# Routing of two expert layers: raw rows gathered and normalised tile by tile, picks in two parts, one-hot products of ids alone

## The chip, the cores and the metric

One NeuronCore of a Trainium2 chip runs the whole program; nothing is exchanged with other cores. Its engines are TensorE (PE, with its weight loads as PEld), VectorE (DVE), ScalarE (ACT), GpSimd (POOL) and SyncE (SP). SP and POOL mostly issue DMAs. The metric is the device time of one execution in microseconds, as the median of several runs.

## The reference

Two layers, each a graph attention over 3327 nodes of 256 features and then a mixture of eight experts, each added to x. Only the second half of a layer matters here:

```python
# layer 0: h = layernorm(x), H = 512
logits = h @ gate_w + gate_b;  probs = softmax(logits)
top2_vals, top2_idx = top_k(probs, 2)
x = x + sum over e of cw[:, e] * (gelu(h @ W1[e] + b1[e]) @ W2[e] + b2[e])     # cw: the two values, 0 elsewhere
# layer 1: xt = layernorm(x), normalised a second time per token, H = 1024
top_p, top_idx = top_k(softmax(xt @ Wr + br), 2);  weights = top_p / top_p.sum()
xe = xn * ln_g[e] + ln_b[e]
x = x + sum over the two picks of weight * (gelu(xe @ W1[e] + b1[e]) @ W2[e] + b2[e])
```

## The kernel before, in words

The nodes are padded to 3328 rows, held in X as T = 26 row tiles of 128 rows (PAIRS = 13 pairs). Attention fills X. Then the class `Experts` does, in each layer, **routing** and the **run of tiles**.

Routing (`route_tensor`, `route_scalar`, `route_vector`, `route_sync`) goes through these stages:

- *Gates.* For each row tile PE turns 128 rows (L2165, two transposes), ACT copies the turned tile out of PSUM (L2128), and PE multiplies it by the gate weights into 8 columns of bank 2 (L2173). Two buffers alternate, so PE turns tile t before it multiplies tile t - 1. After each tile PE does two products that nobody reads (`idle_products`, L2180). ACT's square root for the layer norm (L2432) stands after the tenth tile in ACT's order and needs the variance from DVE (L2424). Meanwhile DVE normalises all of X in place, tile by tile (L2008), and SP stores the result to the DRAM tensor `xs` in two halves (L1966), between the first and the last four of eight loads of the second expert weights W2.
- *Picks.* DVE takes all 26 x 8 logits, finds the two largest of each row with a chain of 17 instructions (L2021 to L2038), each waiting for the one before it (`step`). PE fills the time with 48 unread products, then counts rows per expert (L2189, L2190).
- *Places.* From the counts DVE works out for each pick the tile (of 59) and the place in it (of 128): L2040 to L2065. PE does 96 unread products.
- *One-hots.* The 52 columns of picks go in four quarters c of 13. For each, DVE compares tile numbers (L2102, 13 x 59), compares places (L2107, 13 x 128) and multiplies the first by the row ids (L2111); ACT multiplies the first by the pick's weight (L2151, 13 instructions). PE's 13 products (L2199) put ids and weights side by side, 118 columns, into bank 5. Between the second and the third quarter DVE makes the table of each tile's expert (L2081 to L2087); on it wait the loads of W1. DVE turns bank 5 into `slot_row` (L2118, L2120) and copies the weights to `slot_w` (L2122).

The run has 59 tiles (RUN_TILES). POOL gathers 128 rows of `xs` into one of four `rx` buffers (L2255), PE turns them (L2292), ACT copies (layer 0, L2340) or scales (layer 1, L2344), PE does the hidden products (L2285), ACT the gelu (L2362), PE the second product (L2324), DVE adds the bias and multiplies by the weight (L2388, L2391), and POOL adds the rows to DRAM (L2273). SP loads W1 of tile g + 2 (L2215) once tile g's hidden products are done. In PE's order tile g means: hidden products of g + 1, turning of g + 2, second product of g. The bias b2 (L2225) is loaded once both first gathers have landed, because it lies where X was.

In layer 0 a loop on SP (`gelu_sync`, L1344) stores each finished pair of X to `xd`; in layer 1 `route_sync` stores X to `out` when most of the rows are final (L1953).

## Time and profile before

| | us |
|---|---|
| median of 3 runs (1788.11 to 1790.72) | 1789.14 |
| the profiled execution | 1787.74 |
| its span, first to last instruction | 1786.0 |
| PE busy / DVE busy / ACT busy / POOL busy | 1660.1 / 931.6 / 955.8 / 351.8 |
| mean granted TensorE clock, share of full speed | 0.981 |
| layer 0: gates, picks, places, one-hots (422.5 to 481.4) | 58.9 |
| layer 1: the same stages (1281.9 to 1342.4) | 60.5 |

The profiled execution's own time is 1.74 us longer than its span and 1.4 us shorter than the median. A stage below is a stretch of the span; "busy" in it is the time in which an engine had an instruction. PE counts as busy during the unread products too, so its share does not say where time can be saved.

### The profile page before, as it was taken

The numbers are of one execution on the slowest core, as the hardware profiler recorded it, in microseconds if no ns is written. First come the engines' busy times: TensorE is split into PE (matmuls) and PEld (weight loads), VectorE is DVE, ScalarE is ACT, GpSimd is POOL, SyncE is SP. The second block draws the span as 40 slices with busy tenths as digits, with TensorE's granted clock in tenths as the row PEclk, the third lists the DMA queues.
The fourth block names the chain that finished last, engine by engine and source line by source line (L and its number), as shares of the span: only waits on it lengthen the run. The fifth ranks groups of instructions, "written<-read, shape, count | busy, mean of one in ns | idle before, by whom it ended". The sixth has DMA issues, their size and how long they took to land.

```text
span 1786.0 us, 41369 instructions
## 1 busy us (share of the span) xinstructions
PE 1660.1 (93%) x13364; PEld 1535.9 (86%) x13365; DVE 931.6 (52%) x2186; ACT 955.8 (54%) x2194; POOL 351.8 (20%) x314
## 2 busy tenths in 40 slices
PE   4799999999799999589999999999988999999998
PEld 3588888878789999479999999999978999999997
DVE  4578868778612222568888878877780111111111
ACT  1143444435334433368989989899743444444443
POOL 2110000000156666320000000000002333333332
PEclk9899999999899999799999999999999999999999
DMA  9990000003478887400000000000375666666664
GB/s 160 108 176 10 10 10 9 28 28 125 143 190 208 229 209 186 159 10 18 14 14 19 9 19 18 10 19 14 110 281 175 176 177 179 182 186 186 176 176 97
DMA packets 86495, 189.98 MB, mean 106 GB/s; under 512 B 13737, under 2 KB 60585, under 8 KB 77577
## 3 DMA queue, kind: packets, MB, share of 16 engines
q1 hardware_dynamic: 53705, 139.39, 23.5%
q0 software_dynamic: 31360, 48.45, 17.2%
q10 hardware_dynamic: 1344, 1.05, 0.2%
q8 instruction: 47, 0.77, 0.2%
q14 instruction: 39, 0.32, 0.1%
HBM read 188.98 MB, written 33.11 MB: 124 GB/s over the span
## 4 chain that ended last, share of the span: by engine, by line
PE 52%; DVE 3%; ACT 1%; issue 1%; DMA 1%; DVEq 0%; POOL 0%; ACTq 0%; POOLq 0%
PE bank L1774 24%; PE bank L2285 12%; PE bank L2324 11%; PE bank L707 1%; PE bank L710 1%; PE bank L2292 1%; ACT arena L1476 1%; DVE arena L1612 0%; PE bank L2173 0%; PE bank L697 0%; DVE arena L1610 0%; DMA arena<-xe 0%; DVE X L2107 0%; PE bank L2180 0%; PE bank L2165 0%
## 5 line engine op out<-in xcount | busy, mean ns | idle before, releaser
L1774 PE MATMUL bank<-arena 128*128 128x195 bf16 x5408 | 467.1, 248 | 14.2 <-DVE arena L1612 10.9
L1774 PEld LDWEIGHTS bank<-arena 128*128 128x128 fp8e4 x5408 | 463.8, 97 | 17.6 <-issue 16.7
L1476 ACT ACTIVATE arena<-arena,m_row 128x512 fp8e5<-128x512 f32 (+1 forms) x672 | 401.5, 678 | 44.5 <-DVE arena L1612 32.8
L2285 PEld LDWEIGHTS bank<-X,arena 128*128 128x128 f32 x2832 | 337.1, 194 | 8.7 <-issue 2.3
L2388 DVE TENSOR_TENSOR arena<-bank,X 128x256 f32<-128x256 f32 x118 | 50.1, 425 | 563.7 <-PE bank L2324 563.7
L2285 PE MATMUL bank<-X,arena 128*128 128x128 f32 x2832 | 339.2, 277 | 0.1
L2324 PE MATMUL bank<-arena,X 128*128 x1416 | 325.2, 379 | 2.5 <-ACT X L2362 2.0
L1319 PE MATMUL bank<-arena 128*128 (+1 forms) x1352 | 312.1, 386 | 15.1 <-DVE arena L1225 15.1
L1319 PEld LDWEIGHTS bank<-arena 128*128 128x128 f32 x1352 | 252.5, 191 | 55.7 <-issue 20.9
L2324 PEld LDWEIGHTS bank<-arena,X 128*128 128x128 f32 x1416 | 259.9, 190 | 33.7 <-issue 3.1
L2362 ACT ACTIVATE X<-bank,arena 128x128 f32<-128x128 f32 x708 | 196.0, 379 | 70.2 <-issue 61.5
L1177 ACT ACTIVATE bank<-arena,s_all 128x384 f32<-128x384 f32 (+1 forms) x234 | 133.7, 573 | 185.7 <-DVE arena L1217 182.7
L1217 DVE SCALAR_TENSOR_TENSOR arena<-arena,d_all,bank 128x384 f32<-128x384 f32 (+1 forms) x234 | 140.8, 602 | 67.9 <-PE bank L1319 66.7
L2344 ACT ACTIVATE X<-bank,arena 128x128 f32<-128x128 f32 x118 | 47.6, 454 | 226.8 <-PE bank L2292 226.8
L2207 POOL IOTA arena<- 128x128 f32 x2 | 0.5, 238 | 808.4 <-DVEq L1674 495.0
L1610 DVE SCALAR_TENSOR_TENSOR arena<-arena 128x512 uint32<-128x512 uint32 (+1 forms) x168 | 109.7, 653 | 73.4 <-PE bank L1774 53.9
L2273 POOL DMA_INDIRECT out<-X,slot_row x59 | 93.4, 1583 | 269.2 <-DVE X L2391 266.2
L2255 POOL DMA_INDIRECT arena<-xs,slot_row x118 | 116.3, 986 | 146.6 <-DVE slot_w L2122 111.2
L1225 DVE TENSOR_TENSOR arena<-arena 128x384 f32<-128x384 f32 (+1 forms) x234 | 126.9, 546 | 0.0
L1612 DVE SCALAR_TENSOR_TENSOR arena<-arena 128x512 uint32<-128x512 uint32 (+1 forms) x168 | 108.9, 648 | 0.0
L2340 ACT COPY X<-bank 128x256 f32<-128x256 f32 x59 | 22.0, 373 | 105.0 <-PE bank L2292 105.0
L2292 PE MATMUL bank<-ident,arena 128*128 128x128 f32 x236 | 46.2, 278 | 11.5 <-DMA arena<-xs,slot_row 9.0
(249 smaller groups left out, 1346.2 us busy)
## 6 DMA issues: line engine op xcount, KB each, us to landing
arena<-m1w SPq DMA_DIRECT2D x67, 1024.0 KB, 10.6
arena<-m0w SPq DMA_DIRECT2D x67, 512.0 KB, 7.1
xs<-X SPq DMA_DIRECT2D x4, 1664.0 KB, 7.1
arena<-qd SPq DMA_DIRECT2D x25, 256.0 KB, 3.1
arena<-adjT POOLq DMA_DIRECT2D x13, 448.0 KB, 12.9
arena<-adjT POOLq DMA_DIRECT2D x13, 384.0 KB, 10.8
xe<-zeros POOLq DMA_DIRECT2D x1, 3456.0 KB, 21.7
X<-x_in SPq DMA_DIRECT2D x2, 1664.0 KB, 11.5
```

Source lines behind the costliest of these rows:

```text
L1177: a.activation(self.exp_bank[s][:, 0:nt * P], self.rows[r][:, 0:nt * P], ACT.Exp, bias=s_all[:, at(c, 1)]).then_inc(self.exp_ready[s], 1)
L1217: v.scalar_tensor_tensor(out=self.prob[q][:, 0:w], in0=self.rows[r][:, W:W + w], scalar=d_all[:, at(c, 1)], in1=self.exp_bank[s][:, 0:w], ...
L1225: v.tensor_tensor(self.prob[q][:, 0:w], self.prob[q][:, 0:w], mask[:, at(c * NP + b * W, w)], ALU.min).then_inc(self.prob_ready[q], 1)
L1319: last = pe.matmul(bank[3 * r + n][:, 0:D + 1], self.prob[q][:, n * P:(n + 1) * P], V[:, at(c * VW, D + 1)], start=False, stop=False, skip ...
L1476: last = a.activation(self.sign[slot].bitcast(F8W)[:, q * W:q * W + nt * P], self.row[r][:, 0:nt * P], ACT.Sigmoid, scale=STEEP, bias=self ...
L1610: v.scalar_tensor_tensor(out=pos, in0=sg, scalar=1, in1=m, op0=ALU.logical_shift_left, op1=ALU.bitwise_and).then_inc(self.pos_ready, 1)
L1612: v.scalar_tensor_tensor(out=neg, in0=sg, scalar=0x08080808, in1=m, op0=ALU.bitwise_xor, op1=ALU.bitwise_and).then_inc(self.neg_ready[slot ...
L1774: last = pe.matmul(bank[rb * NT + n][:, kind * KW:(kind + 1) * KW], self.split[slot][kind].bitcast(F8)[:, q * W + n * P:q * W + (n + 1) * ...
L2255: pool.indirect_dma_start(self.rx[g % 4], None, xs[:, :], bass.IndirectOffsetOnAxis(ap=slot_row[:, g:g + 1], axis=0)).then_inc(self.rx_loa ...
L2285: last = pe.matmul(bank[2 * s + c // 4][:, c % 4 * P:(c % 4 + 1) * P], self.W1[s][:, k * HID + c * P:k * HID + (c + 1) * P], self.rxt[s][: ...
L2324: last = pe.matmul(bank[5 + s][:, 0:D], self.ht[s][:, c * P:(c + 1) * P], self.W2[:, at(e * (HC * D) + c * D, D)], start=(c == 0), stop=(c ...
L2362: last = a.activation(self.ht[s][:, c * P:(c + 1) * P], bank[2 * s + c // 4][:, c % 4 * P:(c % 4 + 1) * P], ACT.Gelu, bias=self.b1[:, at(e ...
```

## The change

- `norm` of X in place (L2008) and its stores are gone. SP stores the raw rows to `xs`: in layer 0 a second store beside each store to `xd`; in layer 1 in three parts (12, 12 and 2 tiles), each together with a store to `out`, the first as soon as three blocks of rows are final.
- A row of `xs` grows from 256 to 260 words (ROW): four words `row_cols` hold the row's scale and shift, the first pick's weight, and the second's minus the first's. They are stored by one DMA in 16-byte pieces, once `weights()` is done.
- DVE normalises each gathered tile in the run (`norm`), two instructions, three tiles ahead; PE turns a tile after that.
- Picks are found in two parts, tiles 0 to 19 and 20 to 25; the second part's logits go to bank 7.
- The one-hot products carry ids alone, 59 columns. Of 13 id products DVE does 3 (in one instruction), ACT 10. A second pick's id is raised by 4096, from which DVE reads afterwards whether a slot is a second pick.
- The table of experts moves behind the last quarter, `weights()` from the first to the second quarter.
- The two unread products after each gate are gone; 48 become 20 and 96 become 88.

```diff
@@ gelu_sync (layer 0)
                     sp.dma_start(xd[...], X[...]).then_inc(self.x_kept, 16)
+                    sp.dma_start(xs[at(i * 2 * P, 2 * P), 0:D].rearrange("(t p) d -> p t d", p=P),
+                                 X[...]).then_inc(rows_stored, 16)
@@ route_sync
-                    for a, b, final in ((0, T - 2, 6), (T - 2, T, 7)):
+                    for a, b, final in ((0, 12, 3), (12, 24, 6), (24, T, 7)):
                         sp.wait_ge(rows_final, final)
+                        sp.dma_start(xs[a * P:b * P, 0:D]..., X[...]).then_inc(self.rows_stored, 16)
                         sp.dma_start(total[a * P:b * P, :]..., X[...]).then_inc(self.x_spilled, 16)
...
-                load_w2(range(4))
-                for g in range(2):
-                    sp.wait_ge(self.x_scaled, (g + 1) * PAIRS)
-                    sp.dma_start(xs[...], X[...]).then_inc(self.xn_stored[g], 16)
-                load_w2(range(4, 8))
+                for g in range(8):
+                    sp.dma_start(self.W2[...], w2m[...]).then_inc(self.w2_loaded, 16)
+                sp.wait_ge(self.weights_ready, 1)
+                sp.dma_start(xs[0:NP, D:ROW].rearrange("(t p) c -> p t c", p=P), self.row_cols
+                             ).then_inc(self.cols_stored, 16)
@@ route_vector
-                with v.Fori(0, PAIRS) as i:
-                    for s in range(2):
-                        v.tensor_scalar(xv, xv, self.scale_x[...], self.shift_x[...], ALU.mult, ALU.add)
+                for (a, b), logits_bank in zip(PICK_PARTS, (bank[2], bank[7])):
+                    pick_part(a, b, logits_bank)
...
+                v.wait_ge(*x_stored)
+                v.wait_ge(self.rows_stored, self.n_stored)
                 for c in range(4):
...
-                    v.tensor_tensor(tiles_[:, :, 0, :], eq, over(ids, G), ALU.mult)
+                    v.tensor_tensor(self.hot_tile[b][:, 0:few * G]..., eq[:, 0:few, :],
+                                    over(ids[:, first:first + few], G), ALU.mult)
-                    if c == 1:
-                        tile_table()
+                tile_table()
...
-                v.tensor_copy(slot_w[:, :], bank[5][:, G:2 * G])
+                step(v.tensor_scalar(slot_w[:, :], slots, float(SECOND), None, ALU.is_ge))
+                step(v.scalar_tensor_tensor(out=self.spare, in0=slot_w[:, :], scalar=-float(SECOND), ...))
@@ route_tensor
-                    idle_products(2)
...
-                idle_products(48)
-                pe.wait_ge(self.picked, 3)
+                idle_products(20)
+                pe.wait_ge(self.picked, 6)
...
-                idle_products(96)
+                idle_products(88)
@@ tiles_gpsimd
-                for s in range(2):
-                    pool.wait_ge(self.xn_stored[s], 16)
+                pool.wait_ge(self.rows_stored, self.n_stored)
+                pool.wait_ge(self.cols_stored, 16)
@@ tiles_tensor
-                        pe.wait_ge(self.rx_loaded[(q + 2) % 4], 16 * (j + 1 + (q >= 2)))
+                        pe.wait_ge(self.rx_ready, g + 3)
                         turn_x((q + 2) % 4)
@@ tiles_vector
+                def norm(g, s, nth):
+                    x = self.rx[s]
+                    v.wait_ge(self.rx_loaded[s], 16 * nth)
+                    v.scalar_tensor_tensor(out=slot_w[:, at(g, 1)], in0=slot_w[:, at(g, 1)], scalar=x[:, D + 3:D + 4],
+                                           in1=x[:, D + 2:D + 3], op0=ALU.mult, op1=ALU.add)
+                    v.tensor_scalar(x[:, 0:D], x[:, 0:D], x[:, D:D + 1], x[:, D + 1:D + 2], ALU.mult, ALU.add
+                                    ).then_inc(self.rx_ready, 1)
...
                     v.tensor_scalar(self.ry[s], self.ysum[s], slot_w[:, at(g, 1)], None, ALU.mult)
+                    norm(g + 3, (q + 3) % 4, j + 1 + (q >= 1))
```

Where instructions move on an engine, in the order in which the program holds them ("waits" names semaphores; `x0_` is the expert stage).

DVE, layer 0, the one-hot quarters before (equal tiles L2102, weights L2075 to L2077, places L2107, ids L2111, table of experts L2081 to L2087):

```order
L2102 TENSOR_TENSOR arena<-tile_no,arena 128x767 [waits x0_hot_used0,x0_xn_stored0,x0_places_ready,x0_route]
L2075 TENSOR_REDUCE arena<-arena 128x26 [waits x0_exps]
L2076 RECIPROCAL arena<-arena 128x26 [waits x0_route]
L2077 TENSOR_TENSOR arena<-arena 128x26 [waits x0_route]
L2107 TENSOR_TENSOR X<-arena 128x1664
L2111 TENSOR_TENSOR X<-arena,row_id 128x13x59 [waits x0_hot_equal0]
L2102 TENSOR_TENSOR arena<-tile_no,arena 128x767 [waits x0_xn_stored1,x0_hot_used1]
L2107 TENSOR_TENSOR X<-arena 128x1664
L2111 TENSOR_TENSOR X<-arena,row_id 128x13x59 [waits x0_hot_equal1]
L2081 TENSOR_TENSOR arena<-arena,tile_no 1x472
L2085 TENSOR_REDUCE arena<-arena 1x59 [waits x0_route]
```

The same stretch with the change (equal tiles L2107, places L2112, ids L2119, weights L2080 to L2083):

```order
L2107 TENSOR_TENSOR arena<-tile_no,arena 128x767 [waits x0_rows_stored,a0_x_kept,x0_hot_used0,x0_places_ready,x0_route]
L2112 TENSOR_TENSOR X<-arena 128x1664
L2119 TENSOR_TENSOR X<-arena,row_id 128x177 [waits x0_hot_equal0]
L2107 TENSOR_TENSOR arena<-tile_no,arena 128x767 [waits x0_hot_used1]
L2080 TENSOR_REDUCE arena<-arena 128x26 [waits x0_exps]
L2082 RECIPROCAL arena<-arena 128x26 [waits x0_route]
L2083 SCALAR_TENSOR_TENSOR arena<-arena 128x26 [waits x0_route]
L2112 TENSOR_TENSOR X<-arena 128x1664
L2119 TENSOR_TENSOR X<-arena 128x177 [waits x0_hot_equal0]
L2088 TENSOR_TENSOR arena<-arena,tile_no 1x472
```

The ids shrink from 767 to 177 columns, the weights go a quarter later, the table goes behind the fourth quarter, and the waits for the stores stand ahead of the first quarter.

DVE, layer 0, one tile of the run's loop, before (bias L2388, weight L2391; then the next tile's expert is loaded, L2384):

```order
L2388 ISA [waits x0_added1,x0_y_ready1]
L2388 TENSOR_TENSOR arena<-bank,X 128x256
L2390 REGISTER_ALU
L2391 REGISTER_ALU [waits x0_ysum_ready]
L2391 TENSOR_SCALAR X<-arena,slot_w 128x256
```

And with the change (bias L2411, weight L2414, then `norm`, L2394 and L2396):

```order
L2411 ISA [waits x0_added1,x0_y_ready1]
L2411 TENSOR_TENSOR arena<-bank,X 128x256
L2414 TENSOR_SCALAR X<-arena,slot_w 128x256 [waits x0_ysum_ready]
L2394 ISA [waits x0_rx_loaded2]
L2394 SCALAR_TENSOR_TENSOR slot_w<-slot_w,arena 128x1
L2396 TENSOR_SCALAR arena<-arena 128x256
```

Two instructions and a wait for a gather come between a tile's last DVE work and the next tile's first.

## Rows read from the trace of the kernel before

**Rows 1.** Stages: us; busy PE, PEld, DVE, ACT, POOL (count); clock, DMA share, GB/s.

```profile
444.90:451.40 6.50, 5.45 (x50) 4.63 (x48) 5.98 (x18) 0.62 (x2) 0.00 (x0) 1.00 0.86 263
459.10:481.40 22.30, 17.12 (x134) 16.14 (x132) 17.16 (x22) 14.13 (x54) 0.00 (x0) 0.92 0.15 47
493.60:711.00 217.40, 215.02 (x1480) 199.93 (x1481) 44.35 (x114) 87.34 (x289) 142.29 (x111) 1.00 0.83 208
1281.90:1307.20 25.30, 24.40 (x238) 23.12 (x237) 15.67 (x53) 12.30 (x30) 0.24 (x1) 1.00 0.99 355
1307.20:1313.60 6.40, 2.45 (x24) 1.96 (x21) 5.85 (x18) 0.03 (x1) 0.00 (x0) 1.00 0.87 266
1313.60:1321.30 7.70, 7.70 (x56) 6.30 (x57) 6.63 (x28) 0.46 (x2) 0.00 (x0) 0.78 1.02 404
1321.30:1342.40 21.10, 17.37 (x149) 16.06 (x147) 16.94 (x22) 14.13 (x54) 0.00 (x0) 1.00 0.40 156
1353.90:1775.00 421.10, 421.10 (x2903) 396.99 (x2903) 45.14 (x116) 174.48 (x586) 143.64 (x111) 1.00 0.62 177
```

**Rows 2.** Timeline of PE, gates of layer 1: start us, us, [idle before <-releaser].

```profile
1284.19 0.38 PE L2165 MATMUL bank<-ident,X 128*128 128x128 f32 x2
1284.40 0.51 PE L2173 MATMUL bank<-slot_w,arena 128*128 128x8 f32 x4
1284.77 0.38 PE L2180 MATMUL bank<-ident,ones 128*128 128x256 bf16 x2
...
1303.55 0.61 PE L2173 MATMUL bank<-slot_w,arena 128*128 128x8 f32 x4
```

**Rows 3.** Timeline of ACT, gates of layer 1.

```profile
1284.60 0.37 ACT L2128 COPY arena<-bank 128x256 f32<-128x256 f32 x1 [0.43 <-PE bank L2165]
...
1289.79 1.28 ACT L2432 ACT_TABLE_LOAD   x1
```

**Rows 4.** The line that normalises X, both layers: ns min/median/max, first and last start us.

```profile
L2008 DVE TENSOR_SCALAR X<-X,arena x52: 405/410/415, 433.2 to 1306.9; - x52
```

**Rows 5.** Timeline of DVE: variance of layer 0; one step of layer 1's picks.

```profile
431.25 0.18 DVE L2424 TENSOR_SCALAR rstd<-mv 128x26 f32<-128x26 f32 x1
...
1313.06 0.19 DVE L2037 TENSOR_TENSOR arena<-arena 128x26 f32<-128x26 f32 x1
```

**Rows 6.** Timeline of DVE, one-hots of layer 1.

```profile
1328.99 0.63 DVE L2081 TENSOR_TENSOR arena<-arena,tile_no 1x472 f32<-1x472 f32 x1
...
1334.18 0.94 DVE L2102 TENSOR_TENSOR arena<-tile_no,arena 128x767 f32<-128x767 f32 x1
1335.05 1.87 DVE L2107 TENSOR_TENSOR X<-arena 128x1664 f32<-128x1664 f32 x1
1336.85 0.94 DVE L2111 TENSOR_TENSOR X<-arena,row_id 128x767 f32<-128x767 f32 x1
```

**Rows 7.** Timelines of ACT and PE, the last quarter of layer 1.

```profile
1335.15 3.16 ACT L2151 ACTIVATE X<-arena 128x59 f32<-128x59 f32 x13 [0.38 <-DVE arena L2102]
...
1338.46 3.13 PE L2199 MATMUL bank<-X 128*128 128x118 f32 x26 [0.41 <-ACT X L2151]
```

**Rows 8.** DMA page of 198 to 206 us: packets, MB, share of 16 engines.

```profile
q1 hardware_dynamic: 2336, 0.01, 13.5%
```

**Rows 9.** The page's DMA issues: KB each, median us to landing.

```profile
xs<-X SPq DMA_DIRECT2D x4, 1664.0 KB, 7.1
...
xd<-X SPq DMA_DIRECT2D x13, 256.0 KB, 2.1
```

**Rows 10.** Timelines of SP and ACT, first tile of layer 0's run.

```profile
486.37 0.36 SPq L2225 DMA_DIRECT2D X<-m0b  x1
...
493.63 1.14 ACT L2362 ACTIVATE X<-bank,arena 128x128 f32<-128x128 f32 x4 [6.12 <-issue]
```

**Rows 11.** Timelines of DVE and PE, one tile of layer 0's run.

```profile
610.68 0.35 DVE L2391 TENSOR_SCALAR X<-arena,slot_w 128x256 f32<-128x256 f32 x1
...
611.50 0.38 PE L2292 MATMUL bank<-ident,arena 128*128 128x128 f32 x2
```

More of the change, by code:

```diff
@@ L69 @@
 EARLY_PAIR = 8
+ROW = D + 4
+SECOND = 4096
+PICK_PARTS = ((0, 20), (20, T))
+IDS_ON_DVE = 3
 EARLY_GROUPS = 4
@@ L1869, in __init__ @@
                 k += 2 * T
-                self.shift_x = words(k, T)
-                k += T
                 self.scale_x = words(k, T)
@@ L1879, in __init__ @@
                 assert k <= ARENA, (k, ARENA)
-                half, places, tiles_ = PAIRS * D, PAIRS * P, PAIRS * 2 * SLOT_TILES
+                half, places, tiles_ = PAIRS * D, PAIRS * P, PAIRS * SLOT_TILES
                 assert places + tiles_ <= half
@@ L1884, in __init__ @@
                 self.hot_tile = [X[:, s * half + places:s * half + places + tiles_] for s in range(2)]
-                self.equal = [words(weights_at + 2 * KC * hidden + s * tiles_ // 2, tiles_ // 2) for s in range(2)]
-                assert 2 * KC * hidden + tiles_ <= E * KC * hidden
+                self.equal = [words(weights_at + 2 * KC * hidden + s * tiles_, tiles_) for s in range(2)]
+                assert 2 * KC * hidden + 2 * tiles_ <= E * KC * hidden
                 k = b1_at + E * hidden
-                self.rx = [words(k + s * D, D) for s in range(4)]
-                k += 4 * D
+                self.rx = [words(k + s * ROW, ROW) for s in range(4)]
+                k += 4 * ROW
                 self.ysum = [words(k + s * D, D) for s in range(2)]
@@ L1925, in __init__ @@
                 self.places_ready = sem(tag + "places_ready")
-                self.xn_stored = [sem(f"{tag}xn_stored{s}") for s in range(2)]
+                self.rows_stored = sem(tag + "rows_stored")
+                self.n_stored = (3 if second_norm else PAIRS) * 16
+                self.cols_stored = sem(tag + "cols_stored")
                 self.ysum_ready = sem(tag + "ysum_ready")
@@ L2011, in route_vector @@
+                v.scalar_tensor_tensor(out=shift, in0=mv[:, 0:T], scalar=-1.0, in1=scale, op0=ALU.mult, op1=ALU.mult)
+                v.tensor_scalar(self.second_id, row_id[:, :], float(SECOND), None, ALU.add
+                                ).then_inc(self.second_ids, 1)
                 TE = T * E
-                lg3 = self.logits.rearrange("p (t e) -> p t e", e=E)
                 w3 = self.work.rearrange("p (t e) -> p t e", e=E)
-                def spread(a):
-                    return a.rearrange("p (t o) -> p t o", o=1).to_broadcast([P, T, E])
@@ L2377, in tiles_vector, with tile @@
             def tiles_vector(self, v):
+                def norm(g, s, nth):
[5 more added lines that the diff above has]
+                                    ).then_inc(self.rx_ready, 1)
+                v.wait_ge(self.slots_ready, 1)
+                for g in range(3):
+                    norm(g, g, 1)
                 v.wait_ge(self.tiles_known, 1)
-                v.wait_ge(self.slots_ready, 2)
                 v.wait_ge(self.b_loaded, 32)
-                def tile(i, s):
-                    g = 2 * i + s
+                def tile(j, q):
+                    g, i, s = 4 * j + q, 2 * j + q // 2, q % 2
                     e = v.value_load(expert_of[0:1, at(g, 1)], min_val=0, max_val=E - 1)
@@ L2392, in tile @@
                                     ).then_inc(self.ry_ready[s], 1)
-                for s in range(2):
-                    tile(0, s)
-                with v.Fori(1, RUN_TILES // 2) as i:
-                    for s in range(2):
-                        tile(i, s)
-                tile(RUN_TILES // 2, 0)
+                    if not isinstance(g, int) or g + 3 < RUN_TILES:
+                        norm(g + 3, (q + 3) % 4, j + 1 + (q >= 1))
+                for q in range(4):
+                    tile(0, q)
+                with v.Fori(1, RUN_TILES // 4) as j:
+                    for q in range(4):
+                        tile(j, q)
+                for q in range(3):
+                    tile(RUN_TILES // 4, q)
         def all_stats(v, stat):
```

173 lines of the change are left out of this document (88 added, 85 removed).

## The prediction

> **What bounds the kernel now.** I read three views in this order: busy time by stage, the timelines inside the routing stages, and the timelines of the run of tiles. In the stage rows [rows 1] the reader is to see two kinds of stretch. In the runs PE is busy 215.0 of 217.4 us (layer 0) and 421.1 of 421.1 us (layer 1): nothing there can get faster by this change, only slower. In routing PE's busy time is partly unread products and says nothing; there one chain passes from engine to engine, and what it takes off comes off the kernel. The two routings take 58.9 and 60.5 us, so they are what the change can win from.
>
> Inside them: layer 1's gates run at PE's own pace, 0.21 us of turning, 0.37 of logits and 0.21 of unread products, 0.80 a tile [rows 2], with ACT idle 0.43 before each copy [rows 3]. The last logits start at 1303.55 [rows 2], yet the stage ends at 1307.2 [rows 1], because DVE is still normalising X (26 instructions of 410 ns and their register work, the last at 1306.9) [rows 4]. The picks are one DVE chain; the one-hots are DVE's too, 0.87 + 1.80 + 0.87 us from start to start in a quarter, 3.54 in all [rows 6], against 3.16 of ACT and 3.13 of PE [rows 7].
>
> **The change part by part.** *Gates, layer 1.* Without unread products PE needs 0.58 a tile. The copy starts 0.41 after the turning, 0.03 after its end, and lasts 0.37 [rows 2, 3]; with 0.03 to hand back, logits can start 0.81 after the turning, and PE would be there after 0.79. So the pace is about 0.60, and 26 tiles give 5.2 us. The table load of 1.28 for the square root [rows 3] has less ACT idleness to hide in, minus 0.2. The last logits end at 1299.0 instead of 1304.0, the twentieth tile's (six tiles of 0.60 before) at 1295.5. The normalising of X goes; what was behind it in DVE's order starts at once.
>
> *Picks.* 17 instructions took 6.4 us [rows 1], 0.376 each at 208 columns; at 26 columns one takes 0.19 plus 0.03 to hand over [rows 5]. In between on a straight line: 0.35 at 160 columns, 0.24 at 48. Both parts have 16 instructions, two of them partly overlapped: 5.4 and 3.7 us. Layer 1: 1295.5 + 5.4 + 3.7 = 1304.6 against 1313.6, **-9.0**. Layer 0: the square root needs a variance that is ready at 431.43 [rows 5], which the faster gates don't move; PE comes there sooner and waits some 2 us. With the root and one copy (0.2 + 0.4) it goes on at 432.05; the last 16 tiles take 9.3, so gates end at 441.4, part one starts at 437.9, and picks end at 447.0 against 451.4, **-4.4**.
>
> *Places* stay, 7.7 us [rows 1].
>
> *One-hots.* A quarter costs DVE 0.87 + 1.80 + 0.25 (ids of 3 x 59 columns, by the same line as above) = 2.92. The table of experts (1.7 us: four steps, the first two 0.63 [rows 6]) goes behind the last quarter, beside PE. Until the fourth compare: three quarters, the weights (0.65; 0.85 in layer 0) and 0.95, then ACT's 10 of 13 products, 10 x 0.243 = 2.43 [rows 7], then PE's last 13. Those take 3.13 at 118 columns [rows 7]; at 8 columns 13 would take 2.4 (0.37 for two) [rows 2]; 59 lies between, I take 2.75 and keep both ends (-0.35 to +0.4 per layer). Sum 8.76 + 0.65 + 0.95 + 2.43 + 2.75 = 15.6, and 1.2 for four small steps to `slot_row` (two more than before): 16.8 against 21.1 in layer 1, **-4.3**; 17.0 against 22.3 in layer 0, **-5.3**.
>
> *Stores and waits.* The new DVE waits ahead of the first quarter ask for the raw rows. In layer 0 they go out pair by pair, now two stores each on SP's queue. One lands in 2.1 [rows 9]; even one after the other the last six pairs' twelve would take 25 from the end of attention at 422.5 on, to 448, and the quarters start at 454.6: hidden; if not, DVE and all behind it wait. W2 no longer has the row stores in its middle, and its 4 MB are done by then. In layer 1 half the rows leave during attention, where the queue is idle. SP waits for the weights, and behind it in its queue stand b1 and the loads of W1; these wait for the table of experts anyway, 9 us later, so 0. The 3328 pieces of 16 bytes: a store of 2336 packets of 4 bytes kept the engines busy for 13.5% of 8 us [rows 8], 1.1 us spread over 16; by that, 1.5 us plus issuing and landing, perhaps 6. Were a piece as dear as a row of 1 KB (two stores of 1664 rows landed in 7.1 each [rows 9]), 14. There are 12 us between weights and gather: I take 0, nearest to the small packets, with 2 us as the upper end. The Trainium skill (DMA: Bandwidth & Descriptors, Specifications) says that below 512 B a transfer is read-modify-write and not at line rate; it gives no price, and the packets of that store show none.
>
> *First gather.* In layer 0 the first gelu at 493.63 has waited 6.12 us although its products were long done: for b2, issued at 486.37 when the first gathers had landed [rows 10]. `norm` (about 0.65) hides behind that load; if it were gone, 0.65. In layer 1 products end the wait, so 0.65 counts, and the gather now meets the loads of W1, which start only 2 us before it: 0.5 more. I take **+0.3** and **+1.2**.
>
> *Run, layer 0.* 1480 PE instructions at 26 a tile are 57 tiles of 3.81 us. With the change DVE does two more instructions right after a tile's weighting, and PE's next turning waits for them. Today the weighting starts at 610.68, ends at 611.03, and the turning starts at 611.50 [rows 11], 0.47 later, of which 0.11 is its weight load. The normalising takes 0.41 [rows 4], the one-column instruction before it 0.1 to 0.2 (0.19 at 26 columns [rows 5]); a DVE instruction starts 0.07 before the last one's recorded end [rows 6]. So the row is ready 0.43 to 0.6 after the weighting, and PE waits 0.05 to 0.25 a tile. I take 0.08, since alternate tiles have 0.1 more room: 4.6 us, of which 1.6 takes the place of the 2.4 that PE idles there already [rows 1]: **+3.0**, between 0 and 14. In layer 1 the hidden products last twice as long and cover it: 0.
>
> *Gathered rows.* 1040 bytes instead of 1024 add 1.6% to the gathers, 131 KB of the 208 GB/s x 3.81 us = 793 KB that a tile moves in layer 0. No row of this trace shows rows that start off a round address, so I bound it: by bytes 0, and by the 0.17 of DMA share that is left in layer 0's run [rows 1], still no wait of PE as long as a gather takes less than twice as long. The Trainium skill (same page, How a descriptor splits into AXI transactions) speaks against the change here: a piece not starting on 256 bytes is read from the boundary below it, which makes five transactions of such a row where an aligned 1024 bytes takes four; by that rule a gather grows by a quarter and the sum by nothing, and no run here shows it yet.
>
> Sum: layer 1 -9.0 - 4.3 + 1.2 = -12.1; layer 0 -4.4 - 5.3 + 0.3 + 3.0 = -6.4. Together **-18.5 us** on the profiled 1787.7, 1769.2; its time lies 1.4 under the median, so the median becomes **1770.6**.
>
> **The rivals.** *A. The turnings of layer 0's run come late.* If `norm` ends 0.25 a tile late instead of 0.08, the run pays 57 x 0.25 = 14 and not 3: about 1781. For it: the narrow 0.47; against it: the sequencer can prepare `norm` while DVE still weights.
>
> *B. The clock.* After 4 us of idle PE before the counts of layer 1, the granted clock of the next 7.7 us is 0.78 [rows 1], which is 3.4 us at 1.2 instead of 2.4 GHz. The change removes cover at three places: PE stands some 2 us in layer 0's gates and 3.5 us in both picks (1 us in layer 0 before). At half clock the gates there lose 1.7; the unread products behind the counts may end late and hold the first quarter by 1: together 3 to 5, about 1775.
>
> *C. Slower than before: the gathers land late.* `norm` for tile g + 3 stands in DVE's order ahead of the next tile's bias, so a late gather now stops DVE as well as PE. A DMA engine is busy 0.83 of layer 0's run [rows 1], and W1 is wanted just as it lands. Each 0.1 us that a tile is late costs 5.7; it becomes slower than no change from about 0.39 a tile on (18.5 + 3.6 over 57), where it gives 1793. It needs gathers that take some 1.5 us longer in the queue, against which stand the 16 bytes. The rule on off-boundary pieces just named would work in this direction.
>
> *D. The routing doesn't shorten as said*, because another wait takes its place (the four words land late, the raw rows hold the first quarter, the first run tile waits for W1): half of it, about 1780.
>
> *E. No waits in the run of layer 0 and narrow products at their shortest:* about 1766.
>
> **How the numbers follow.** Forecast 0.60, A 0.14, B 0.10, C 0.04, D 0.07, E 0.05. Forecast with its own bounds is 1766 to 1775. The range reaches down to E with the lower ends, 1763, and up to A and D, 1781; it leaves out C and the far ends. A measurement of this kernel can tell 0.2%, 3.6 us: all but C and a bad D are faster by more. Faster 0.93, same 0.03, slower 0.04.
>
> **What would show it.** Right: gates at 0.60 a tile; counts some 9 us earlier in layer 1 and 4 in layer 0; quarters of 2.9 us with PE's last products within 3 us of ACT's; gathers starting about 13 and 10 us earlier; layer 0's tiles at 3.8 to 3.9 us with a small wait of the turning for DVE. Wrong: turnings that wait 0.2 us or more for DVE (A), a clock below 0.8 in layer 0's gates or over the first quarter (B), DVE's `norm` waiting for gathers in the loop (C), or gathers that start long after `slot_row` (D).

## The result, and the profile after

The changed kernel took 1839.97 us (median of 4 runs, 1838.84 to 1843.87) against 1788.75 for the kernel before beside it: 1.0288 times as long, 95% interval 1.0270 to 1.0306. The forecast was 1770.6, in a range of 1763 to 1781. The profiled execution took 1840.67 us over a span of 1838.9 (before: 1786.0), at a mean granted clock of 0.956 (before: 0.981).

Stages of the changed kernel, in the columns of [rows 1]. The rows are layer 0's gates, part two of its picks, its quarters, and its run; then layer 1's gates, quarters and run.

```profile
422.20:451.20 29.00, 28.76 (x160) 27.92 (x159) 14.25 (x47) 12.51 (x30) 0.38 (x2) 0.57 0.66 232
451.20:454.90 3.70, 3.70 (x19) 2.64 (x18) 3.17 (x16) 0.18 (x2) 0.00 (x0) 0.50 0.00 0
...
463.10:485.40 22.30, 19.94 (x132) 19.07 (x129) 15.14 (x23) 11.31 (x42) 0.00 (x0) 0.74 0.22 51
496.30:757.00 260.70, 231.04 (x1487) 203.59 (x1486) 69.79 (x226) 87.17 (x289) 144.64 (x111) 1.00 0.71 175
1328.90:1356.90 28.00, 27.76 (x161) 26.89 (x159) 11.32 (x43) 12.20 (x30) 0.24 (x1) 0.59 1.01 381
...
1368.90:1393.50 24.60, 22.24 (x126) 21.68 (x123) 14.93 (x23) 11.30 (x42) 0.00 (x0) 0.63 0.31 81
1407.00:1828.10 421.10, 421.10 (x2904) 396.99 (x2903) 70.46 (x228) 174.04 (x586) 146.06 (x112) 1.00 0.62 177
```

The reader is to see two losses. Layer 0's run, 217.4 us before with PE idle 2.4 of it [rows 1], is 260.7 with PE idle 29.7, at full clock. And the gates, picks and quarters of both layers run at a granted clock of 0.50 to 0.74, although PE is busy 28.76 of 29.00 us in the gates. Layer 1's run is the same to the tenth.

*The gates.* Timeline of PE in layer 0 (start us, us); the gates of before are [rows 2].

```profile
431.12 0.67 PE L2176 MATMUL bank<-ident,X 128*128 128x128 f32 x2
431.58 0.86 PE L2186 MATMUL bank<-slot_w,arena 128*128 128x8 f32 x4
432.29 0.67 PE L2176 MATMUL bank<-ident,X 128*128 128x128 f32 x2
```

From tile to tile 1.17 us; the forecast was 0.60, before it was 0.80. In its first tiles, while the granted clock is still full, the pace is 0.62 and 0.73 in turn, as here in layer 1:

```profile
1330.25 0.42 PE L2176 MATMUL bank<-ident,X 128*128 128x128 f32 x2
1330.87 0.41 PE L2176 MATMUL bank<-ident,X 128*128 128x128 f32 x2
1331.60 0.42 PE L2176 MATMUL bank<-ident,X 128*128 128x128 f32 x2
```

The trace's clock records show half clock (1.2 GHz) from 426.2 to 456.9 and from 473.9 to 494.4 in layer 0, from 1334.1 to 1361.4 and from 1375.1 to 1405.8 in layer 1.

*The quarters.* Timeline of PE, layer 0:

```profile
466.68 3.08 PE L2210 MATMUL bank<-X 128*128 128x59 f32 x26 [0.66 <-ACT X L2162]
469.95 3.11 PE L2210 MATMUL bank<-X 128*128 128x59 f32 x26 [0.19 <-DVE X L2119]
473.40 10.83 PE L2210 MATMUL bank<-X 128*128 128x59 f32 x52 [0.34 <-ACT X L2162]
```

A quarter has 13 products, which the trace shows as 26 records. The first two quarters take PE as long as one at 118 columns did, 3.13 [rows 7]; the last two take 10.83 where they would take about 6.4.

*The run of layer 0.* Timeline of one tile, PE and DVE; [rows 11] show the same place before. L2296 are the hidden products, L2303 the turning, L2335 the second product.

```profile
608.98 1.95 PE L2296 MATMUL bank<-X,arena 128*128 128x128 f32 x16
...
610.22 0.21 DVE L2394 SCALAR_TENSOR_TENSOR slot_w<-slot_w,arena 128x1 f32 x1
610.35 0.41 DVE L2396 TENSOR_SCALAR arena<-arena 128x256 f32<-128x256 f32 x1
...
610.81 0.44 PE L2303 MATMUL bank<-ident,arena 128*128 128x128 f32 x2
...
611.81 1.99 PE L2335 MATMUL bank<-arena,X 128*128 x8 [0.56 <-issue]
...
613.64 1.95 PE L2296 MATMUL bank<-X,arena 128*128 128x128 f32 x16
```

Before, the turning of 611.50 [rows 11] is followed by

```profile
611.72 1.89 PE L2324 MATMUL bank<-arena,X 128*128 x8
```

With the change the turning starts 0.05 after `norm` ends. The second product starts 1.00 after the turning, where before it was 0.22; "issue" says that it waited for nothing that the profile shows as a semaphore. What PE's sequencer (PEldq) did meanwhile stands under the line of `value_load`, the read of the tile's expert number into a register, L2331, in the view of one line (608 to 618 us):

```profile
L2331 PEldq TENSOR_LOAD <-expert_of x2: 297/298/300, 610.9 to 615.5; - x2
L2331 PEldq SEQ_ASSERT  x2: 18/18/18, 611.5 to 616.0; - x2
```

And before (L2320, the same window):

```profile
L2320 PEldq TENSOR_LOAD <-expert_of x3: 311/506/632, 609.9 to 617.5; - x3
```

With the change it read the expert's number at 610.9, behind the end of `norm`. Over 55 tiles of the run the read starts 0.15 to 0.20 us after `norm` has ended, and the next weight load of the second product starts 0.86 (median) after the read. Before, the read started 1.6 us (median of 53 tiles) ahead of the turning, at 609.9 in the tile shown, under the hidden products.

### The profile page after: what moved, and what is told of

Its sections match the earlier page's. It is cut to its first block, busy times and chain, and to the rows that moved or that the text cites. A ratio compares the mean times of both kernels' runs of the same rounds, so it can differ in the third digit from the quotient of the medians.

```text
span 1838.9 us, 41113 instructions
## 1 busy us (share of the span) xinstructions
PE 1694.1 (92%) x13188; PEld 1558.6 (85%) x13189; DVE 967.5 (53%) x2404; ACT 949.9 (52%) x2170; POOL 356.1 (19%) x314
## 4 chain that ended last, share of the span: by engine, by line
PE 52%; DVE 2%; ACT 1%; issue 1%; DMA 1%; POOL 0%; ACTq 0%; DVEq 0%; POOLq 0%
PE bank L1781 23%; PE bank L2296 12%; PE bank L2335 11%; PE bank L711 1%; PE bank L714 1%; PE bank L2210 1%; PE bank L2186 1%; PE bank L2303 1%; ACT arena L1483 1%; PE bank L2176 1%; DVE arena L1619 0%; DMA arena<-xe 0%; PE bank L701 0%; DVE arena L1617 0%; PE bank L2192 0%
## 5 line engine op out<-in xcount | busy, mean ns | idle before, releaser
L1483 ACT ACTIVATE arena<-arena,m_row 128x512 fp8e5<-128x512 f32 (+1 forms) x672 | 401.7, 678 | 44.5 <-DVE arena L1619 32.5
L2335 PE MATMUL bank<-arena,X 128*128 x1416 | 330.4, 383 | 29.3 <-issue 28.8
L2296 PEld LDWEIGHTS bank<-X,arena 128*128 128x128 f32 x2832 | 338.1, 194 | 6.5 <-issue 0.7
L2296 PE MATMUL bank<-X,arena 128*128 128x128 f32 x2832 | 338.7, 277 | 0.3 <-DMA arena<-m0w 0.3
L2411 DVE TENSOR_TENSOR arena<-bank,X 128x256 f32<-128x256 f32 x118 | 50.1, 424 | 546.6 <-PE bank L2335 546.6
L2335 PEld LDWEIGHTS bank<-arena,X 128*128 128x128 f32 x1416 | 259.7, 190 | 73.1 <-issue 42.5
L2355 ACT ACTIVATE X<-bank,arena 128x128 f32<-128x128 f32 x118 | 47.6, 453 | 234.9 <-PE bank L2303 226.2
L2303 PE MATMUL bank<-ident,arena 128*128 128x128 f32 x236 | 47.8, 285 | 13.6 <-DVE arena L2396 11.2
## 6 DMA issues: line engine op xcount, KB each, us to landing
arena<-m1w SPq DMA_DIRECT2D x67, 1024.0 KB, 11.8
X<-x_in SPq DMA_DIRECT2D x2, 1664.0 KB, 11.6
```

Source lines behind the costliest of these rows:

```text
L1483: last = a.activation(self.sign[slot].bitcast(F8W)[:, q * W:q * W + nt * P], self.row[r][:, 0:nt * P], ACT.Sigmoid, scale=STEEP, bias=self ...
L2296: last = pe.matmul(bank[2 * s + c // 4][:, c % 4 * P:(c % 4 + 1) * P], self.W1[s][:, k * HID + c * P:k * HID + (c + 1) * P], self.rxt[s][: ...
L2335: last = pe.matmul(bank[5 + s][:, 0:D], self.ht[s][:, c * P:(c + 1) * P], self.W2[:, at(e * (HC * D) + c * D, D)], start=(c == 0), stop=(c ...
```

## The experiments

Stage lengths of every profiled run, from the starts of PE's instructions: gates and picks (first turning to counts), quarters (counts to the first turning of the run), start (to the first second product), run of layer 0 (first to last second product). Layer 1's run is 419.4 to 419.5 us in all of them. The profiled runs enter the routing of layer 0 at 421.6 to 426.1 us, so stages compare better than spans. The change, e2 and e8 have the same routing instructions, yet their quarters differ by up to 2.5 us (34.9 to 37.4, 34.2 to 36.7), so that much in a stretch where the clock falls shows nothing.

| run | L0 gates, picks | quarters | start | run | L1 gates, picks | quarters | start | median us |
|---|---|---|---|---|---|---|---|---|
| before | 28.9 | 33.8 | 9.8 | 219.3 | 31.7 | 32.0 | 11.7 | 1788.75 |
| the change | 33.1 | 34.9 | 7.4 | 262.7 | 32.0 | 36.7 | 12.8 | 1839.97 |
| e1 unread back | 27.7 | 34.9 | 8.5 | 262.7 | 27.6 | 34.3 | 12.5 | 1830.85 |
| e2 early read | 32.3 | 37.4 | 8.5 | 222.8 | 32.9 | 34.2 | 13.0 | 1801.52 |
| e3 both | 27.7 | 35.0 | 8.2 | 221.9 | 27.6 | 34.1 | 12.8 | 1790.25 |
| e4 before, gates bare | 35.3 | 33.2 | 9.1 | 220.1 | 34.6 | 33.0 | 11.5 | 1801.57 |
| e5 e3, 118 columns | 27.7 | 30.8 | 7.3 | 222.6 | 27.6 | 32.9 | 12.6 | 1781.12 |
| e6 e5, norm first | 27.7 | 30.7 | 7.9 | 224.8 | 27.6 | 32.5 | 11.8 | 1783.34 |
| e7 e6, one unread | 35.2 | 30.7 | 8.0 | 225.0 | 25.4 | 32.1 | 11.6 | 1792.39 |
| e8 norm first alone | 33.3 | 37.3 | 8.4 | 225.2 | 32.2 | 36.7 | 12.6 | 1807.29 |
| e9 e5, W1 later | 27.7 | 30.2 | 12.1 | 224.0 | 27.6 | 29.1 | 12.7 | 1781.77 |
| e10 e5, scale first | 27.6 | 30.9 | 7.6 | 219.5 | 27.6 | 32.9 | 11.6 | 1778.87 |
| e11 e9 and e10 | 27.7 | 30.2 | 10.1 | 221.2 | 27.6 | 29.4 | 12.2 | 1779.60 |
| e12 e10, W1 later in layer 1 | 27.6 | 30.7 | 7.3 | 219.8 | 27.6 | 29.2 | 12.6 | 1777.22 |

### e1: the unread products back

```diff
                     last.then_inc(self.lg_done, 1)
+                    idle_products(2)
...
-                idle_products(20)
+                idle_products(48)
...
-                idle_products(88)
+                idle_products(96)
```

> The changed kernel with the unread products put back: 2 behind each tile's logits, 48 ahead of the counts and 96 behind them. Theory (the routing lost its gain because PE's granted clock fell to half beside the gates and over the one-hots): no stretch below full clock in either layer's gates and hardly one over the one-hots; counts about 6 us earlier than in the changed kernel in layer 0 (449 instead of 455.2), from the counts to the first turning of the run 29 to 30 us instead of 34.9 (layer 0) and 36.7 (layer 1); the run of layer 0 keeps its 263 us. Time 18 to 28 us below the changed kernel, about 1815, still slower than before. Rival (the routing is late for another cause: the 16-byte stores, the two-part picks, ACT's larger share): the clock comes back and the stages keep their lengths, time within 5 us of the changed kernel.

Measured 1830.85 us (1.023 times before, 1.0209 to 1.0251). Stages of gates and quarters, layer 0:

```profile
423.10:445.60 22.50, 21.60 (x211) 20.62 (x210) 13.70 (x45) 12.10 (x30) 0.38 (x2) 1.00 0.85 300
462.00:480.00 18.00, 17.23 (x104) 16.83 (x104) 10.76 (x17) 8.86 (x32) 0.00 (x0) 0.70 0.27 61
```

The gates are back at full clock and their old length, the counts 5.4 and 4.4 us earlier. The quarters stay at 0.70, so the fall there has a cause of its own. The expectation was right for the gates and wrong for the quarters: 9.1 us were won where it had 18 to 28.

### e2: the expert's number read ahead of the wait

```diff
+                    e = pe.value_load(expert_of[0:1, at(g, 1)], min_val=0, max_val=E - 1)
                     if left >= 2:
                         pe.wait_ge(self.rx_ready, g + 3)
                         turn_x((q + 2) % 4)
-                    e = pe.value_load(expert_of[0:1, at(g, 1)], min_val=0, max_val=E - 1)
```

> The changed kernel with one line moved: PE's sequencer reads the tile's expert number ahead of its wait for the normalised row instead of behind the turning. Nothing of the arithmetic or of the waits themselves changes. Theory (the run of layer 0 is longer because the wait for the normalised row, which now passes only as the hidden products end, holds the in-order sequencer, so that the 0.3 us read of the expert number and the address arithmetic behind it run after the turning and PE idles before the second product): the idle time ahead of the second product goes from about 0.5 us a tile to under 0.1, the tile from 4.5 to 3.8 us, the run of layer 0 from 262.7 to 219 to 226 us, the time 36 to 43 us below the changed kernel, about 1800. Rival (the turning itself is late for DVE, or the off-boundary gathers are slow): the run stays above 250 us and the time falls by less than 10 us.

Measured 1801.52 us (1.0072, 1.0047 to 1.0097), 38.5 below the change; the run of layer 0 is 222.8. Timeline of PE:

```profile
609.68 1.95 PE L2296 MATMUL bank<-X,arena 128*128 128x128 f32 x16
611.51 0.44 PE L2303 MATMUL bank<-ident,arena 128*128 128x128 f32 x2
611.78 1.94 PE L2335 MATMUL bank<-arena,X 128*128 x8
613.55 1.95 PE L2296 MATMUL bank<-X,arena 128*128 128x128 f32 x16
```

The second product follows the turning by 0.27 instead of 1.00, and the tile takes 3.87 instead of 4.66. One moved line, with the same waits and the same arithmetic, gives back nearly the whole loss of the run: the theory holds.

### e3: both

> Both edits together: unread products back, and the expert number read ahead of the wait. Theory: the two causes are independent, so the gains add: 54 to 71 us below the changed kernel, 1769 to 1786, faster than before. Rival (one cause with two faces, or the clock falls elsewhere once the run is shorter): the sum falls short by 10 us or more, above 1790.

Measured 1790.25 us (1.0000, 0.9988 to 1.0012): 49.7 below the change and no faster than before. The two gains add (9.1 and 38.5 make 47.6), but the expected 54 to 71 had counted on the quarters, whose second half stays at half clock.

### e4: the kernel before without its unread products beside the gates

```diff
                     last.then_inc(self.lg_done, 1)
-                    idle_products(2)
```

> The kernel before with one line out: no unread products beside the gates; the 48 and 96 around the counts stay. Theory (those products alone held the clock): granted clock at half in the gates of both layers, logits paced at about 1.1 us a tile instead of 0.80, gates 6 to 8 us longer, and the one-hots behind them longer too; 10 to 25 us slower than before in all, about 1800 to 1812. Rival (the clock needs more than that change, for instance the gap that DVE's shorter normalising opened or the smaller counts of unread products): gates at 0.60 a tile and full clock, 0 to 9 us faster than before, since the normalising of X still ends the stage.

Measured 1801.57 us (1.0058, 1.0036 to 1.0080). Stage of layer 0's gates:

```profile
426.10:454.40 28.30, 28.05 (x159) 27.28 (x158) 19.01 (x56) 12.41 (x30) 0.38 (x2) 0.58 0.50 172
```

The products that nobody reads were what kept the clock up in the gates: without them the stretch from first turning to counts grows by 6.4 and 2.9 us, and with them back in e1 it shrinks again. The quarters, still at 118 columns, keep their length within 1.1 us, where the expectation had them longer too.

### e5: e3 with one-hot products of 118 columns

```diff
+                        wide = SLOT_TILES * min(2, PAIRS - q)
-                        last = pe.matmul(bank[5][:, 0:SLOT_TILES], ...
-                                         self.hot_tile[c % 2][:, q * SLOT_TILES:(q + 1) * SLOT_TILES],
+                        last = pe.matmul(bank[5][:, 0:wide], ...
+                                         self.hot_tile[c % 2][:, q * SLOT_TILES:q * SLOT_TILES + wide],
```

> Both edits of before (unread products back, expert number read ahead of the wait), and the one-hot products stream 118 columns instead of 59: each reads its pair's 59 and the next pair's 59, which lie beside them and are written by then; the second half of the result is read by nobody. A product took 0.11 us in the records at 118 columns (before) and at 59 (the change), so at full clock the width costs nothing. Theory (PE's granted clock fell in the one-hots because the narrow products keep the array at work for less of the time): the 20 to 24 us at half clock over the last two quarters shrink to the 3 to 7 us that the kernel before shows there; the last two quarters take 6 us instead of 11; from the counts to the first turning of the run 29 to 30 us instead of 35.0 and 34.1; 8 to 11 us below that kernel, about 1780. Rival (the clock falls there for what went before, such as the gap ahead of the first quarter or the quicker quarters): the stretch stays over 15 us and the time within 2 us of 1790.

Measured 1781.12 us (0.9940, 0.9916 to 0.9963), 9.1 below e3. PE's last quarters in layer 0, first in e3:

```profile
469.90 11.16 PE L2211 MATMUL bank<-X 128*128 128x59 f32 x52 [0.34 <-ACT X L2162]
```

and with 118 columns:

```profile
470.11 3.08 PE L2213 MATMUL bank<-X 128*128 128x118 f32 x26 [0.34 <-ACT X L2162]
473.41 3.08 PE L2213 MATMUL bank<-X 128*128 128x118 f32 x26 [0.22 <-ACT X L2162]
```

Halving the columns had saved no time, 3.08 us for a quarter's 13 products (26 records) at either width, and it had cost the clock. Twice the columns, half of them unread, keep it. The rival, that the clock falls in the quarters for what went before, also fails in e4 and e7: there the gates of layer 0 ran at 0.58 and 0.70, and the quarters of 118 columns behind them still took 33.2 and 30.7 us, no longer than behind gates at full clock (33.8 and 30.7).

### e6 and e8: the row normalised ahead of the bias

```diff
+                    if not isinstance(g, int) or g + 3 < RUN_TILES:
+                        norm(g + 3, (q + 3) % 4, j + 1 + (q >= 1))
                     e = v.value_load(expert_of[0:1, at(g, 1)], min_val=0, max_val=E - 1)
                     v.wait_ge(self.y_ready[s], i + 2)
...
-                    if not isinstance(g, int) or g + 3 < RUN_TILES:
-                        norm(g + 3, (q + 3) % 4, j + 1 + (q >= 1))
```

e8 is this edit on the change alone:

> The changed kernel with that one edit alone: the row of tile g + 3 normalised ahead of tile g's bias; the expert number is read behind the turning, as in the changed kernel, and no unread products are put back. Theory (PE's sequencer is held by the wait for the row): the wait passes some 1.2 us earlier, while the hidden products still run, so the read of the expert number hides again without being moved: the run of layer 0 falls from 262.7 to 219 to 224 us and the time by 38 to 44 us, about 1798. Rival (the read's place alone costs the time, whenever the row is ready): the run stays above 250 us.

Measured 1807.29 us (1.0076, 1.0051 to 1.0100), 32.7 below the change, its run 225.2: somewhat less than the 38 to 44 and somewhat over the 219 to 224 that were expected, and far from the rival's 250. Timeline of one tile, and the line of the read (608 to 617 us):

```profile
608.52 0.41 DVE L2396 TENSOR_SCALAR arena<-arena 128x256 f32<-128x256 f32 x1
609.95 0.38 PE L2303 MATMUL bank<-ident,arena 128*128 128x128 f32 x2
610.16 1.89 PE L2335 MATMUL bank<-arena,X 128*128 x8
L2331 PEldq TENSOR_LOAD <-expert_of x2: 299/305/311, 609.1 to 613.1; - x2
```

The read stands where the change put it, and in 51 of 54 tiles it again starts 0.15 to 0.20 us after `norm` has ended. But the row is ready sooner, and the read hides under the hidden products. So the read's place alone costs next to nothing (225.2 us, against 224.8 in e6 with the read ahead of the wait): the late wait ahead of it does. On top of e5 it is e6:

> The same, and in the run DVE normalises the row of tile g + 3 ahead of tile g's bias instead of behind its weighting. Theory: the row lands 1.2 us before DVE now begins on it, and DVE idles there; so the turning no longer waits for DVE, the run of layer 0 loses the 2.5 us that it is still longer than before (221.9 to about 219.5), bias and weighting come about 0.25 us later, which nothing waits for. About 2.5 us less than without it, 1777. Rival (the later bias and weighting delay the next scatter and through it the gathers; or the 1040-byte rows, not DVE, keep the run long): 221 us or more stay, and the time is the same or some us longer.

Measured 1783.34 us (0.9949, 0.9935 to 0.9964), no gain. The waits of 500 to 710 us (waiter, what it waited for, us in total, times, longest):

```profile
PE bank L2306 <- DVE arena L2399: 4.9, 8, 1.1
```

Most tiles take 3.73 us, as before the change, but eight of 53 take 4.1 to 5.5: `norm` has given up its slack to the gather, and a row that lands late now holds PE. The run got 2.2 us longer instead of 2.5 shorter; this expectation failed.

### e7: one unread product a tile

```diff
-                    idle_products(2)
+                    idle_products(1)
```

> The same with one unread product instead of two behind each tile's logits. Theory (the gates run at PE's pace and one product costs 0.1 us a tile): if the clock holds, gates at 0.70 us a tile, 2.6 us less in layer 0 and up to 2.6 in layer 1, 3 to 5 us less in all, 1773. Rival: one product is too little, the granted clock falls to half in the gates, which then take 1.0 us a tile or more, and the time is 8 to 14 us above that with two.

Measured 1792.39 us (1786.49 to 1803.11; 1.0020, 0.9999 to 1.0041). Stages of the two gates:

```profile
421.60:449.90 28.30, 26.86 (x185) 26.21 (x184) 14.33 (x48) 12.53 (x30) 0.38 (x2) 0.70 0.68 238
1287.80:1308.20 20.40, 19.32 (x187) 18.55 (x186) 10.32 (x40) 11.85 (x30) 0.24 (x1) 1.00 1.02 366
```

Both answers in one execution: in layer 1 the clock holds and 2.2 us are won, in layer 0 it falls and 7.5 are lost. The ten executions spread over 16.6 us and one of them was profiled, so how often either layer loses the clock is not shown. With two unread products it fell in the gates of none of the runs profiled here.

### e9 to e12: the first gathers, and the order within `norm`

e9 issues W1's second load when the first rows have landed:

```diff
-                for s in range(2):
-                    load_w1(s, s)
+                load_w1(0, 0)
                 sp.wait_ge(self.slots_ready, 1)
...
+                sp.wait_ge(self.rx_loaded[0], 16)
+                load_w1(1, 1)
+                sp.wait_ge(self.rx_loaded[1], 16)
```

> The kernel with wide one-hot products (unread products back, early read, 118 columns, rows normalised behind the weighting), and W1's second load issued only when the first gathered rows have landed. Theory (the change moved the table of experts behind the last quarter, so that W1's two loads start 1.2 to 2.7 us ahead of the first gathers and share the DMA engines with them: in layer 1 the first rows came to use 6.5 us after the gather's issue, where it was 2.9 to the turning before): in layer 1 the first rows come 3.2 to 4.5 us after issue, first turning and first hidden products 2 to 3 us earlier, in layer 0 up to 0.7; 2 to 3.5 us less in all, 1778. Rival (the gather is slow for its 1040-byte rows or the 16-byte stores): still 6 us or more after issue, and no gain.

Timeline of DVE in layer 1, `slot_row` and the first `norm`, first in e5:

```profile
1335.23 0.22 DVE L2132 SCALAR_TENSOR_TENSOR slot_row<-bank,arena 128x59 int32<-128x59 f32 x1
1342.36 0.22 DVE L2397 SCALAR_TENSOR_TENSOR slot_w<-slot_w,arena 128x1 f32<-128x1 f32 x1 [6.92 <-DMA arena<-xs,slot_row]
```

and in e9:

```profile
1338.94 0.22 DVE L2132 SCALAR_TENSOR_TENSOR slot_row<-bank,arena 128x59 int32<-128x59 f32 x1
1342.31 0.22 DVE L2397 SCALAR_TENSOR_TENSOR slot_w<-slot_w,arena 128x1 f32<-128x1 f32 x1 [3.15 <-DMA arena<-xs,slot_row]
```

DVE's wait for the first gather fell from 6.92 to 3.15 us: W1's loads had been in its way. But the total, 1781.77 us (0.9947, 0.9931 to 0.9962), did not move, since layer 0 gave the gain back. Its first gelu waits 8.47 us there:

```profile
493.41 1.14 ACT L2376 ACTIVATE X<-bank,arena 128x128 f32<-128x128 f32 x4 [8.47 <-issue]
```

It waits for b2, which now shares the DMA engines with W1's second load: 9.4 us from issue to landing, 4.9 in e5; in both the gelu starts 1.2 us after that landing.

e10 is e5 with the row normalised first and its weight worked out behind (in the loop; the first three tiles keep their order):

```diff
-                    v.scalar_tensor_tensor(out=slot_w[:, at(g, 1)], ...)
                     v.tensor_scalar(x[:, 0:D], x[:, 0:D], ...).then_inc(self.rx_ready, 1)
+                    v.scalar_tensor_tensor(out=slot_w[:, at(g, 1)], ...)
```

> The kernel with wide one-hot products, and in the run DVE normalises the row first and works out the row's weight behind it, instead of the other way round. Theory (what is left of layer 0's longer run, 222.6 against 219.3 us, is the turning's wait for DVE, 1.2 us recorded and as much again in the weight loads): the row is ready 0.14 to 0.2 us earlier a tile, and the run of layer 0 falls to 219.5 to 221; 1.5 to 3 us less in all. Rival (the rest is the gathers' longer rows): the run stays at 222 or more.

Measured 1778.87 us (0.9942, 0.9926 to 0.9958); layer 0's run falls from 222.6 to 219.5, what it was before. The rest of its length had been the turning's wait for DVE, and the longer rows cost nothing that can be seen. The total doesn't show this gain clear of noise: measured each against the kernel before beside it, e5 and e10 stand at 0.9940 and 0.9942.

> Both of these edits together: 3.5 to 6.5 us below the kernel with wide one-hot products (1781), 1775 to 1778, 0.7 to 0.9% faster than before. Rival: no more than the better one of the two.

e11 took 1779.60 us (0.9931, 0.9918 to 0.9945): no more than e10, as the rival said, for the gelu of layer 0. e12 is e11 with layer 0's loads where e10 has them:

```diff
                 load_w1(0, 0)
+                if not self.second_norm:
+                    load_w1(1, 1)
```

> The kernel that normalises the row first (unread products back, early read, 118 columns), with W1's second load behind the first gathered rows in layer 1 alone; layer 0 keeps both loads ahead. Theory (with the load moved in both layers, layer 1 won 3.7 us from the counts to the first turning and layer 0 gave back 4.8 between its first turning and first second product, for there the hidden products of one tile are too short to cover the later load): layer 1 keeps the 3.7, layer 0 its 7 to 8 us: about 1775.5, 0.75 to 0.95% faster than before. Rival (the two runs differ by the attention ahead of them, not by the load): 1778 to 1780.

Measured 1777.22 us (0.9932, 0.9919 to 0.9946). The stages came as expected, 29.2 us for layer 1's quarters and 7.3 for layer 0's start; the median lies 1.7 over the expectation. The reason given there for layer 0 (hidden products too short) was wrong; it was b2. This version is faster than both kernels, by 0.7% and 3.4%; against e10 the intervals overlap, and that step is shown by the stages alone.

## Why the prediction was wrong, by its own steps

By the stages of the table, differences to before in us:

| term | predicted | the change | e12 |
|---|---|---|---|
| layer 0, gates and picks | -4.4 | +4.2 | -1.3 |
| layer 0, quarters and first gather | -5.0 | -1.2 | -5.5 |
| layer 0, run | +3.0 | +43.4 | +0.5 |
| layer 1, gates and picks | -9.0 | +0.3 | -4.1 |
| layer 1, quarters and first gather | -3.1 | +5.8 | -1.9 |
| sum | -18.5 | +52.5 | -12.3 |

The measured sum (+52.5) lies 71.0 us over the forecast (-18.5): 40.4 of it in the run of layer 0, 17.9 in the gates and picks of both layers, 12.7 in their quarters and first gathers.

- **The run of layer 0 is the step that failed worst.** It priced what the turning waits for DVE, and that was right: with the read out of the way (e2) the run is 222.8, 3.4 more than before where 3.0 was forecast. What it left out stands behind the waiting instruction on its own engine. `value_load` and the address arithmetic come after the turning in PE's order; once the wait lasted until the hidden products were nearly over, they lost the cover of those products, and 57 tiles paid about 0.7 each (262.7 against e2's 222.8). The order of PE's instructions is the same in both kernels; only the wait in it became late. The Trainium skill (Perfetto Trace Analysis, Tensor Engine Instruction (MATMUL, LD_WEIGHTS)) has the sequencer push a waiting instruction into a queue and go on to the next. In this trace the read began only when the wait had passed, in all 55 tiles, and in e8, where the wait passed earlier, the read came earlier with it. The measurement decides.
- **The gates: a pace of 0.60 from rows at full clock.** It took for granted that fewer products leave the rest at their speed. The granted clock fell to half, the pace became 1.17. Even at full clock it was 0.68 in the mean (0.62 and 0.73 in turn), so 0.08 a tile was missing from the 0.60 as well. Rival B, one of whose signs was a clock below 0.8 in layer 0's gates, had the right mechanism at the wrong place and size: it looked for the clock where PE stands idle and allowed 1.7 us, while PE was busy 28.76 of 29.00. Against the forecast the two stretches of gates and picks cost 8.6 and 9.3 us.
- **The picks** were right where they can be read off: part two of layer 0 ran from 451.21 to 454.86, 3.65 us against 3.7.
- **The quarters**: DVE's start to start was 2.93 (463.09 to 466.02) as forecast. PE's 13 products took 3.08 to 3.11, not 2.75: the interpolation by width had no basis, and the upper end that it kept was the value. At half clock PE became the bound, and the first quarter to `slot_row` took 22.3 instead of 17.0; in e5, at full clock, 17.8.
- **The first gather** was mis-sized in layer 1: 0.5 for meeting W1's loads, 3.8 measured (6.92 against 3.15). In the change itself this hardly shows, since the slow quarters let W1 pass.
- **Right at zero**: the stores and waits. DVE's first quarter followed the places without a wait; the 3328 pieces of 16 bytes landed 5.5 to 5.8 us after issue, where "perhaps 6" was said. The rule of the Trainium skill (DMA: Bandwidth & Descriptors, Specifications) on transfers below 512 B shows in no wait here. The rule on pieces off 256 bytes (same page, How a descriptor splits into AXI transactions) would make five transactions of a row where an aligned one takes four, an estimate of up to a quarter more for a gather. The trace doesn't show that: the POOL queue, gathers and scatters together, took 36.2% of the engines for 13.68 MB before and 37.4% for 13.92 MB in e10, over 500 to 700 us, 1.5% more per MB, and a gather's packets took 161 ns in the median at 4160 bytes where they took 159 at 4096.
- **Rivals A, C, D and E**: A named the right place, the turnings of layer 0's run, but not the cost: the turning waited no longer than the forecast had it (e2 leaves 3.4), and the loss came behind it. C did not happen in the change, where a row lands 2.6 us or more before `norm` in most tiles; e6, with the slack gone, shows its mechanism. None of D's waits shows in the change: what the first gathers waited for last was `slot_row` from DVE, and the routing stayed long for the clock. E had the narrow products at their shortest; they took 3.08 at full clock, no less than at 118 columns.

What remains open: in the quarters only the width of the products was varied, so why 59 columns lose the clock there and 118 keep it is not shown; whether e7's two answers depend on what ran ahead of the gates was not tried.

## What to carry to other kernels

When a wait on an in-order engine becomes late, price everything behind it in that engine's order, register reads and address arithmetic too, not only the instruction that waits. Before taking out or narrowing products on TensorE, look at the granted clock: here PE fell to half while it was busy 28.76 of 29.00 us, and in the quarters taking 59 of 118 columns away saved no time and lost the clock. A load that moves later meets other transfers: look whose wait it lengthens, in each layer by itself.

## What was not expected of the hardware

- PE busy 28.76 of 29.00 us in the gates at a granted clock of 0.57, and busy 21.60 of 22.50 at 1.00 with two products of 256 columns a tile more: in these rows the busy share does not tell the clock.
- 13 one-hot products (26 records) take 3.08 us at 59 columns and at 118, and 5.4 (half of 10.83) at half clock.
- PE's register read starts only after a semaphore wait that stands ahead of it in its order has passed (0.15 to 0.20 us after `norm` in 55 tiles of the change), and 0.86 us pass from the read to the next weight load that needs it.
